# A graph network kernel with its setup reordered: key store by ScalarE, scale ahead of the step counts, checks partly on Pool, field inside the block loop, edge sums cleared by ScalarE

## What is computed

```python
edge_index = jnp.stack([src, dst])
h = jnp.maximum(_layernorm(x), 0.0)
# round 0: sums over the edges of h[src] and of the edge features
agg_src  = segment_sum(h[src], dst, N)
agg_edge = segment_sum(edge_attr_128, dst, N)
x = x + relu(concatenate([h, agg_src, agg_edge], axis=1) @ W.T + b)
h = jnp.maximum(_layernorm(x), 0.0)
# rounds 1 and 2: mean over the edges, then two dense layers
h = relu((segment_sum(h[src], dst, N) / deg) @ W1_l + b1 + h @ W1_r)
x = x + relu((segment_sum(h[src], dst, N) / deg) @ W2_l + b2 + h @ W2_r)
```

## Time and profile before

| what | value |
|---|---|
| median of 3 runs | 1465.26 us (1460.28 to 1466.94) |
| the profiled execution | 1467.45 us |
| its span, first to last instruction | 1465.7 us |
| granted TensorE clock, mean | 0.976 of full |
| TensorE busy | 1364.9 us, 93% |
| VectorE busy | 817.0 us, 56% |
| Pool busy | 656.8 us, 45% |
| ScalarE busy | 485.4 us, 33% |

### The profile page before, as it was taken

The page is one execution under the profiler, slowest core; times in us unless marked ns, Lnnn a source line. Parts: engine busy times, 40 slices in busy tenths (PEclk is TensorE's granted clock), DMA queues, the critical chain, the costliest instruction groups (busy, mean ns, idle before and its releaser), DMA issues.

```text
span 1465.7 us, 34654 instructions
## 1 busy us (share of the span) xinstructions
PE 1364.9 (93%) x12165; PEld 1232.6 (84%) x12166; DVE 817.0 (56%) x1839; ACT 485.4 (33%) x1388; POOL 656.8 (45%) x770
## 2 busy tenths in 40 slices
PE   3686999999999999998999999999999999899986
PEld 3565999999999999997888888888888888788875
DVE  7678998888888888882545455422222222112111
ACT  2450123456678888881332323211111110000000
POOL 4410000011112122126777777077777726777773
PEclk9698999999999999999999999999999999999998
DMA  6107778888889898885564647456566746657662
GB/s 179 27 4 214 202 219 230 238 249 241 260 261 274 265 278 256 265 263 196 168 223 159 232 139 227 151 185 214 185 214 194 203 155 205 222 178 227 206 171 74
DMA packets 284747, 295.13 MB, mean 201 GB/s; under 512 B 19445, under 2 KB 250048, under 8 KB 284656
## 3 DMA queue, kind: packets, MB, share of 16 engines
q1 hardware_dynamic: 235541, 213.75, 46.7%
q0 software_dynamic: 26016, 69.24, 16.7%
q10 hardware_dynamic: 23099, 10.89, 2.6%
HBM read 245.70 MB, written 48.11 MB: 200 GB/s over the span
## 4 chain that ended last, share of the span: by engine, by line
PE 74%; POOL 11%; issue 6%; DVE 5%; ACT 2%; DMA 1%; ACTq 0%; DVEq 0%; POOLq 0%
PE edge_banks L1036 30%; PE edge_banks L1001 19%; PE banks L975 11%; POOL shared L813 11%; PE edge_banks L1067 3%; PE edge_banks L997 3%; PE banks L1054 3%; ACT shared L1210 1%; PE banks L891 1%; PE edge_banks L1043 1%; ACT banks L1205 1%; PE banks L1048 1%; DMA shared<-g_rows,list_src 1%; DVE edge_t L1370 1%; DVE g_even L1434 0%
## 5 line engine op out<-in xcount | busy, mean ns | idle before, releaser
L813 POOL DMA_INDIRECT shared<-g_rows,list_src x555 | 541.8, 976 | 235.1 <-issue 167.8
L1036 PE MATMUL edge_banks<-g_even,shared 128*128 128x257 f16 (+1 forms) x3822 | 445.4, 273 | 5.4 <-DMA shared<-counts 4.5
L1036 PEld LDWEIGHTS edge_banks<-g_even,shared 128*128 128x128 fp8e3 x3822 | 372.7, 98 | 64.3 <-issue 4.7
L1001 PE MATMUL edge_banks<-shared 128*128 128x128 f32 x2744 | 339.9, 276 | 0.0
L1001 PEld LDWEIGHTS edge_banks<-shared 128*128 128x128 f32 x2744 | 323.6, 193 | 0.0
L792 POOL DMA_DIRECT2D counts<-shared x156 | 76.4, 490 | 473.5 <-ACT shared L1210 458.4
L1588 DVE SCALAR_TENSOR_TENSOR shared<-edge_banks,shared,own 128x128 f32<-128x128 f32 x98 | 34.4, 351 | 374.3 <-PE edge_banks L1036 335.8
L1036 PE MATMUL edge_banks<-shared 128*128 128x256 f16 x1911 | 225.8, 272 | 0.9 <-DVE own L1570 0.9
L1514 DVE TENSOR_TENSOR shared<-iota,shared 128x3528 f16<-128x3528 f16 x98 | 195.5, 1995 | 48.3 <-PE banks L975 48.2
L1210 ACT ACTIVATE shared<-banks 128x392 uint16<-128x392 f32 x312 | 152.3, 488 | 186.9 <-PE banks L975 177.0
L1036 PEld LDWEIGHTS edge_banks<-shared 128*128 128x128 fp8e3 x1911 | 185.3, 97 | 31.3 <-DVE own L1570 1.2
(11 more groups left out here) (277 smaller groups left out, 987.2 us busy)
## 6 DMA issues: line engine op xcount, KB each, us to landing
shared<-in_edge_attr SPq DMA_DIRECT2D x195, 512.0 KB, 4.5
shared<-counts SPq DMA_DIRECT2D x117, 784.0 KB
counts<-shared POOLq DMA_DIRECT2D x156, 196.0 KB, 3.9
shared<-g_rows,list_src POOLq DMA_INDIRECT x555
shared<-hot_rows SPq DMA_DIRECT2D x20, 304.0 KB, 3.0
g_rows<-g_even SPq DMA_DIRECT2D x1, 3136.0 KB, 15.6
g_rows<-shared ACTq DMA_DIRECT2D x49, 64.0 KB
g_rows<-g_even ACTq DMA_DIRECT2D x49, 64.0 KB
```

Of the source, the lines that this page charges most:

```text
L813: pool.indirect_dma_start(ring_g[use % RING][:, t, 0:2 * D], None, g_rows[r], bass.IndirectOffsetOnAxis(ap=list_src[:, at:at + 1], axis=0) ...
L1001: mm = pe.matmul(edge_wide[bank][:, :, at], ring[:, bank * GROUP_TILES + j, :], hot_dst[u][:, k, (j - 1) * SPREAD:j * SPREAD].unsqueeze(1) ...
L1036: mm = pe.matmul(acc[s][:, 0:wide], stream8[slot][:, order[h], :], G[r % 2][:, order[h], 0:wide], start=h == 0, stop=h == BLOCKS - 1, skip ...
```

## The change

The constants are FIELD_AT, CHECKS_AT, FLAG_AT = 38, 24, 46. The keys are stored by ScalarE's queue instead of SP's. Pool makes the two f16 iota tiles, behind tw_ready. VectorE no longer waits for the norms ahead of bn_stats: it copies them behind the twelfth block. The scales and the layer norm's scale and shift come ahead of the step counts; TensorE serves the counts (its two matmul groups on need16 and on halves, moved as they are) behind the first dense blocks (`t == 1`) instead of ahead of the block loop. The largest check, whether dst is sorted, is a subtraction on Pool behind its last list gather; VectorE reduces it with a maximum behind block 24 and takes the small checks ahead. The field is worked out behind block 38 within the loop, the verdict behind block 46, and the two iota tiles behind the loop. Behind the loop TensorE turns the field ahead of the step rows, ScalarE copies it ahead of its rows, and VectorE prepares the list keys ahead of its copies. edge_t is cleared by a ScalarE ACTIVATE of 6400 columns, behind its second step row and ahead of the list tables. VectorE reads the flag ahead of giving go_ready.

```diff
@@ sync
-            sp.wait_ge(S["keys_ready"], 1)
-            sp.dma_start(keys_table.rearrange("(b p) e -> p b e", p=P), keys).then_inc(S["keys_out"], 16)
@@ gpsimd
             pool.wait_ge(S["tw_ready"], 1)
+            pool.tensor_copy(iota2k, iota_i).then_inc(S["rows_iota"], 1)
+            pool.tensor_copy(iota16[:, :], iota_i[:, 0:IOTA]).then_inc(S["rows_iota"], 1)
             pool.wait_ge(S["keys_out"], 16)
...
+            pool.tensor_tensor(disorder[:, :, 0:P - 1], tile_rows[:, :, 0:P - 1], tile_rows[:, :, 1:P], ALU.subtract).then_inc(S["checks_seen"], 1)
             pool.wait_ge(S["field_ready"], 1)
             for u in range(2):
                 pool.memset(hot_dst[u][:, :, GROUP_TILES * SPREAD:GROUP_HOT], 0.0).then_inc(S["edge_cleared"], 1)
-            pool.memset(edge_t[:, :], 0.0).then_inc(S["edge_cleared"], 1)
@@ tensor
-            pe.wait_ge(S["need_ready"], 1)
...
                 if t > 0:
                     dense(t - 1)
+                if t == 1:
+                    pe.wait_ge(S["need_ready"], 1)
...
-                if t == 6:
+                if t == 9:
                     pe.wait_ge(S["viol_ready"], 1)
...
-            pe.wait_ge(S["tables_ready"], 1)
-            step_row(off_f)
             pe.wait_ge(S["field_ready"], 1)
             for c in range(SCHUNKS):
                 for j in range(min(4, SBLK - 4 * c)):
                     mm = pe.transpose(banks[:, c, j * P:(j + 1) * P], field[:, 4 * c + j, :], ident[:, :])
                 mm.then_inc(S["field_up"], 1)
+            pe.wait_ge(S["tables_ready"], 1)
+            step_row(off_f)
@@ scalar
+            act.wait_ge(S["keys_ready"], 1)
+            act.dma_start(keys_table.rearrange("(b p) e -> p b e", p=P), keys).then_inc(S["keys_out"], 16)
             act.wait_ge(S["consts"], 1)
...
             high(len(TURNS) - 1)
+            for c in (1, 3):
+                act.wait_ge(S["field_up"], c + 1)
+                n = min(512, SPAD - c * 512)
+                act.activation(packed[:, c * 512:c * 512 + n], banks[:, c, 0:n], ACT.Copy).then_inc(S["field_taken"], 1)
             act.wait_ge(S["rows_up"], 3)
...
-            for c in (1, 3):
-                act.wait_ge(S["field_up"], c + 1)
-                n = min(512, SPAD - c * 512)
-                act.activation(packed[:, c * 512:c * 512 + n], banks[:, c, 0:n], ACT.Copy).then_inc(S["field_taken"], 1)
             act.wait_ge(S["step_row_up"], 2)
...
             act.sem_inc(S["step_row_taken"], 1)
+            act.wait_ge(S["checks_seen"], 2)
+            act.activation(edge_t[:, :], zeros16[:, 0:1].broadcast_to([P, NPAD + EDGE_COLS]), ACT.Copy).then_inc(S["edge_cleared"], 1)
             act.wait_ge(S["list_turned"], 1)
@@ vector
-            dve.wait_ge(S["squares_up"], 1)
-            link(dve.tensor_copy(norms[:, 0:4], flat[3][:, 0:4]))
-            dve.sem_inc(S["norms_out"], 1)
-
             dve.wait_ge(S["x_in"], 32)
             for b in range(BLOCKS):
+                if b == 12:
+                    dve.wait_ge(S["squares_up"], 1)
+                    dve.tensor_copy(norms[:, 0:4], flat[3][:, 0:4]).then_inc(S["norms_out"], 1)
                 ins = dve.bn_stats(bn[:, b, :], x_sb[:, b, :])
...
-            link(dve.tensor_copy(iota2k, iota_i))
-            dve.tensor_copy(iota16[:, :], iota2k[:, 0:IOTA])
             dve.wait_ge(S["scales_ready"], 1)
...
             dve.sem_inc(S["norms_ready"], 1)
+            dve.wait_ge(S["std_ready"], 1)
+            link(dve.reciprocal(scale[:, :], std[:, :]))
+            link(dve.scalar_tensor_tensor(out=shift[:, :], in0=mean_var[:, :, 0], scalar=-1.0, in1=scale[:, :], op0=ALU.mult, op1=ALU.mult))
+            dve.sem_inc(S["norm_ready"], 1)
+
+            dve.wait_ge(S["rows8_in"], 16 * (PER + 1))
...
+            dve.sem_inc(S["need_ready"], 1)
...
             dve.wait_ge(S["ends_up"], 1)
             link(dve.tensor_copy(c_end, flat[0][0:HOLDERS, 16:16 + PER]))
+            dve.tensor_scalar(over, c_end, float(NSTEP), None, ALU.is_gt)
+            dve.wait_ge(S["rows_iota"], 3)
...
-                if b == 40:
+                if b == FIELD_AT:
+                    dve.wait_ge(S["gathered"], 16 * SBLK)
+                    link(dve.tensor_tensor(outside, halfwords[:, :, :, 1], w_col.unsqueeze(2).broadcast_to([P, SBLK, P]), ALU.not_equal))
+                    dve.scalar_tensor_tensor(out=field, in0=outside, scalar=OUT_OF_WINDOW, in1=halfwords[:, :, :, 0], op0=ALU.mult, op1=ALU.max
+                                             ).then_inc(S["field_ready"], 1)
+                if b == CHECKS_AT:
+                    dve.wait_ge(S["checks_seen"], 1)
+                    link(dve.tensor_reduce(viol[:, 0:1], disorder.rearrange("p b e -> p (b e)"), AX_X, ALU.max))
...
+                if b == FLAG_AT:
                     dve.wait_ge(S["viol_up"], 1)
...
-                if b == 8:
-                    dve.tensor_copy(iota_a, iota_f[:, 0:LO_A].unsqueeze(2).broadcast_to([P, LO_A, STEPS_ROW]))
-                    dve.tensor_copy(iota_b, iota_f[:, 0:LO_B].unsqueeze(2).broadcast_to([P, LO_B, STEPS_ROW]))
-                    dve.tensor_tensor(disorder[:, :, 0:P - 1], tile_rows[:, :, 0:P - 1], tile_rows[:, :, 1:P], ALU.is_gt)
...
+
+            dve.tensor_copy(iota_a, iota_f[:, 0:LO_A].unsqueeze(2).broadcast_to([P, LO_A, STEPS_ROW]))
+            dve.tensor_copy(iota_b, iota_f[:, 0:LO_B].unsqueeze(2).broadcast_to([P, LO_B, STEPS_ROW])).then_inc(S["checks_seen"], 1)
             dve.wait_ge(S["list_gathered"], 16 * LBLK)
...
             dve.wait_ge(S["cell_half"], 1)
+            cnt[0] += 1
+            dve.tensor_scalar(a_tab, packed, 3, LO_A - 1, ALU.logical_shift_right, ALU.bitwise_and).then_inc(dve_link, 1)
+            go = dve.value_load(flags[0:1, 0:1], min_val=0, max_val=1)
+            dve.wait_ge(dve_link, cnt[0])
             dve.sem_inc(S["go_ready"], 1)
-            go = dve.value_load(flags[0:1, 0:1], min_val=0, max_val=1)
```

More of the change, by code:

```diff
@@ L1403, in _ @@
             dve.sem_inc(S["norms_ready"], 1)
+            dve.wait_ge(S["std_ready"], 1)
[3 more added lines that the diff above has]
+            dve.wait_ge(S["rows8_in"], 16 * (PER + 1))
+            link(dve.tensor_tensor(under, rows8, thr8.unsqueeze(2).broadcast_to([HOLDERS, PER + 1, P]), ALU.is_lt))
@@ new lines, in _ @@
+            link(dve.tensor_reduce(under_n, under, AX_X, ALU.add))
+            link(dve.scalar_tensor_tensor(out=first_e, in0=tw_f, scalar=float(P), in1=under_n, op0=ALU.mult, op1=ALU.add))
+            link(dve.tensor_tensor(in_win, first_e[:, 1:PER + 1], first_e[:, 0:PER], ALU.subtract))
+            link(dve.tensor_scalar(need_i, in_win, float(P - 1), None, ALU.add))
+            link(dve.tensor_scalar(need_i, need_i, 7, None, ALU.arith_shift_right))
+            link(dve.scalar_tensor_tensor(out=need, in0=need_i, scalar=1.0, in1=in_dense, op0=ALU.max, op1=ALU.mult))
@@ new lines, in _ @@
+            dve.tensor_copy(need16, need)
+            link(dve.scalar_tensor_tensor(out=pairs16[:, :, 1], in0=need, scalar=-float(P), in1=in_win, op0=ALU.mult, op1=ALU.add))
+            dve.sem_inc(S["need_ready"], 1)
+            dve.tensor_tensor(disorder[:, :, P - 1], base_col, tile_rows[:, :, 0], ALU.subtract)
+            dve.tensor_tensor(gap[:, 0:LASTB], mark_f[:, 0:LASTB], pair_col[:, 0:LASTB], ALU.subtract)
+            dve.tensor_tensor(gap[0:LASTR, LASTB:TBLK], mark_f[0:LASTR, LASTB:TBLK], pair_col[0:LASTR, LASTB:TBLK], ALU.subtract)
@@ new lines, in _ @@
+            dve.tensor_tensor(gap[0:LASTR + 1, TBLK:TBLK + 1], tile_rows[0:LASTR + 1, LASTB, LEFT - 1:LEFT], pair_col[0:LASTR + 1, LASTB:TBLK], ALU.subtract)
+            dve.tensor_scalar(col_over[:, 0:LASTB], col_raw[:, 0:LASTB], float(EDGE_COLS - SPREAD), None, ALU.is_gt)
+            link(dve.tensor_scalar(col_over[0:LASTR + 1, LASTB:TBLK], col_raw[0:LASTR + 1, LASTB:TBLK], float(EDGE_COLS - SPREAD), None, ALU.is_gt))
+            dve.tensor_scalar(gap_over, gap, float(REACH - 1), None, ALU.is_gt)
@@ L1409, in _ @@
                 dve.tensor_scalar(halves[j % 5][0:HOLDERS, :], iota2k[0:HOLDERS, :], c_end[:, j:j + 1], None, ALU.is_ge).then_inc(S["half_ready"], 1)
-            dve.wait_ge(S["std_ready"], 1)
-            link(dve.reciprocal(scale[:, :], std[:, :]))
-            link(dve.scalar_tensor_tensor(out=shift[:, :], in0=mean_var[:, :, 0], scalar=-1.0, in1=scale[:, :], op0=ALU.mult, op1=ALU.mult))
-            dve.sem_inc(S["norm_ready"], 1)
             dve.wait_ge(S["half_taken"], PER)
@@ L1463, in _ @@
-            dve.wait_ge(S["gathered"], 16 * SBLK)
-            halfwords = gathered.bitcast(U16).rearrange("p (b q k) -> p b q k", q=P, k=2)
-            link(dve.tensor_tensor(outside, halfwords[:, :, :, 1], w_col.unsqueeze(2).broadcast_to([P, SBLK, P]), ALU.not_equal))
-            dve.scalar_tensor_tensor(out=field, in0=outside, scalar=OUT_OF_WINDOW, in1=halfwords[:, :, :, 0], op0=ALU.mult, op1=ALU.max
-                                     ).then_inc(S["field_ready"], 1)
```

(7 more changed lines are left out.)

65 lines of the change are left out of this document (23 added, 42 removed).

## The result

| what | before | after |
|---|---|---|
| median (20 runs each) | 1465.88 us (1460.28 to 1470.99) | 1471.09 us (1467.14 to 1478.1) |
| ratio | | 1.0040, 95% interval 1.0027 to 1.0052 |
| the profiled execution | 1467.45 us | 1475.61 us |
| first instruction of the building | 120.32 us | 124.43 us |

The change costs 0.4%, 5.2 us between the medians, with an interval of 4.0 to 7.6. That is a small loss, but one that these many runs can tell from nothing: my remark that 7.3 us is about what a measurement of this kernel can tell was too wide. 1468 had been forecast, within 0.5% of before, and the result is within it.

A forecast was written before the change was run, and what follows sets the result against it. With TensorE busy 93% of the span, the building's start (120.32 us) was taken to set the end. Terms -0.9 -0.1 -6.8 +3.7 +4.5 +2.1 = +2.5 us gave 1467.75, so 1468; range 1460 to 1474, likeliest case 0.54.

The forecast's parts named there:

- Key store by ScalarE: Setup: the keys stored earlier let Pool's gathers start earlier, worth nothing by itself; 0.
- Start of the statistics: Setup: bn_stats no longer waits for the norms, against some hold by Pool's iota casts; -0.9 us.
- Scale ahead of the counts: Ahead of the loop: VectorE's 4.37 us idle is swapped for a wait in the middle; -0.1 us.
- Checks out of block 8: Loop, block 8: the hole goes, two turns taking 5.25 us instead of 12.01; -6.8 us.
- Checks at block 24: Loop, block 24: VectorE's reduction, a wait for Pool's subtraction and half a clock restart make a hole; +3.7 us.
- Rival C: Loop, block 24: Pool's subtraction holds the loop, deciding from 7.8 us on; 1473 at 8 us; chance 0.09.
- Field at block 38: Loop, block 38: working out the field stalls the loop, with half a clock restart; +4.5 us.
- Loop end 102.6: End of the block loop: 102.16 us before, less 1.0 and 6.8, plus 3.7 and 4.5.
- Tail: Loop's end to building: 20.3 us instead of 18.16, ScalarE's 5.5 us clear standing ahead of the cell table; +2.1 us.
- Rival A: Tail: ScalarE's clear is hidden, so -2.2 us instead of +2.1, in all 1463.5; chance 0.13.
- Rival B: Ahead of and in the loop: TensorE is granted full speed, -1.3 us in all, 1464; chance 0.2.
- Rival D: Loop and tail: checks, field and clear cost nothing where they are put; -12.7 us, 1452.6; chance 0.04.

The follow-up runs named there:

- e5: The changed kernel with step counts and comparisons put back ahead of the layer norm's scale and served ahead of the block loop; ratio to before 1.0013.
- e9: The kernel before with the checks alone moved: Pool subtracts behind its list gathers, VectorE checks behind block 24, iota tiles behind the loop; ratio to before 0.9995.
- e1: The changed kernel with ScalarE's clear of edge_t moved behind the doubling of the cell table; ratio to before 1.0015.
- c0_changed: The changed kernel, unedited, run on another chip; ratio to before 1.0029, building starts at 135.44 us.
- c1_before: The kernel before, unedited, profiled on another chip; building starts at 129.32 us.
- e7: The changed kernel rearranged: counts first, checks and iota tiles ahead of the loop, field behind it, clear behind the cell table, former tail order; ratio to before 0.9945.
- e6: The changed kernel with SP's first four loads of edge features issued once the field is turned, not behind go_ready; ratio to before 1.0027.

## Why the prediction held, point by point

The start of the building was forecast at +2.5 us and came at +4.1; the median was forecast at 1468 and is 1471.09, inside the likeliest case's own range of 1464 to 1472. That it lies so near is in part luck, as two errors in the loop cancel.

*Key store by ScalarE, 0.* The gathers start at 25.01 instead of 26.13 and nobody waits for them. Held.

*Start of the statistics, -0.9.* 25.56 to 24.59, -0.97. L1352 took 1.78 where its like took 0.28 before; it ended as Pool's cast ended. The casts took 1.68 and 0.51 (1.65 and 0.4 forecast). The Trainium skill (SBUF — State Buffer, "Who interferes with whom") says that such an operation of VectorE can take the pair of ports that it shares with Pool, and that one of the two then blocks for the other's whole instruction; by this rule, the trace agrees.

*Scale ahead of the counts, -0.1.* Off by 1.3. The loop starts at 56.31, 0.5 earlier than forecast, but the twelve us from there to block 8 take 12.56 instead of 10.81. The row of TensorE at 57.26 says why: with the first dense blocks done at 48.3, the second set has to wait for VectorE to take the banks (2.19 us idle), and runs at half clock (3.75 us for 8 matmuls, where the second set before took 2.27). At the list's starts both kernels stand at the same time, 64.61 after and 64.69 before. Of the bounds this was the upper one, "the slow clock now falls on the turns behind". e5 agrees: ahead of the loop the order is worth nothing, and with the counts put back the second set runs at full clock and block 8 comes 1.9 us earlier.

*Checks out of block 8, -6.8.* -6.7. Held.

*Checks at block 24, +3.7.* +2.3 (10.18 less 7.87). This term was sized too high. Pool's subtraction took 2.95 us (3.0 forecast) and was over at 78.21, ahead of block 24's L1447 at 79.55: Pool's gathers ended earlier than I had them, and VectorE came later. No wait, and no fall of the clock. The Trainium skill's figure (GPSIMD Engine Reference, "Elementwise — side-by-side cycle accounting") would give 3.6 us, as an estimate from its 4497 ns for 2048 elements; this case's 1.79 ns an element is below its 2.2, and decides. Rival C, that the loop waits for Pool, falls in both kernels that could have shown it (the changed one and e9).

*Field at block 38, +4.5.* +4.4, with the half clock behind it. Held.

*Loop end 102.6.* It was 102.6, by luck: two errors, +1.3 and -1.4, cancel.

*Tail, +2.1.* +3.7: from the first instruction behind the loop to the building 21.9 us instead of 18.25. This is the step that failed in size. Its clear was right (5.54 us, 5.5 forecast; e1 takes 4.9 us off by moving it). What I had not counted is the field's turning at half clock, 3.25 us for 14 instead of 1.75: I had let the slow clock of the field's hole end with the loop. The second step row ends 12.3 us behind the loop instead of 10.5, of which the turning is 1.5, and everything behind it is as forecast. c0_changed bears this out: its field was turned in 1.75 us, and its tail is 2.1 longer than c1_before's. (VectorE was through with its tables 9.0 us behind the loop and not 7; the sum didn't rest on it.) Rival A, a hidden clear, falls in this kernel and is what e1 and e7 make true.

*Rival B, the clock stays up:* it did not, at 56 to 60 and 96 to 106 us. *Rival D, the change does as its words say:* it did not. The three pieces that were put in the loop or on ScalarE cost 2.3, 4.4 and 4.9 us where they were put. e7 puts the checks beside a wait and the clear behind the cell table that the start waits for, and starts the building 11.5 us earlier than c1_before, where D had worked out 12.7.

*From the building's start to the end.* I took it as one to one. The medians differ by 5.2 us where the start differs by 4.1, and that is within the interval. In the profiled pair the end is 8.2 us later, and the difference grows early: TensorE's first group of edge sums starts 4.1 us later, the 20th at 187.55 instead of 180.70, 6.85 later, and the 99th 7.25 later. It stood 1.75 us for edge features ahead of the fifth group, which SP now begins to ask for at 125.10 instead of 119.83, and its clock from 130 to 160 us was 0.89 instead of 0.99. e6 took the late loads away and the total did not follow, so they are not shown to cost anything in the end. What the rest is stays open.

## What to carry to other kernels

Work that was put into this loop of engines in lockstep cost about its full length there, whatever the shares of busy time say; put it beside a wait that is already there. When a long instruction that nobody needs yet moves to another engine, look at what is queued behind it: three instructions further on, the clear costs 4.9 us less at the start of the building. And when TensorE is made to stand, give what it does next a bound at half clock, past the end of the stage; behind one and the same stop it came back in time for the next step in some executions and not in others.

## What the runs showed of the hardware

TensorE's clock does not fall behind every stop. In the changed kernel it stood 3.57 us at block 38 and then ran at 0.50 for 10 us; behind the same stop c0_changed shows 0.68 and 0.50 for 4 us, and full clock from about 114 us. In e9 it stood 3.09 us at block 24, by its timeline, and the clock stayed at 1.00 (4 matmuls in 1.13 us):

```profile
93.28 1.13 PE L892 MATMUL banks<-w_l,edge_t 128*128 128x256 f32 x4 [3.09 <-DVE own L1436]
```

Pool's two-input subtraction, 2.95 us, ran beside VectorE's loop instructions, which read PSUM, and these kept their 0.48 us. In e7 it ran beside the statistics' aggregation, whose last 38 took 2.61 us, as they did in e5 with nothing on Pool. Beside its casts and its clearing memset VectorE's instructions took longer and ended within 0.2 us of them: 1.78 against 0.28 us, and 3.69 against 0.29.
